# Mixture-of-experts tower: token groups prepared further ahead on four row buffers, and routed sums scattered straight into the output

## The reference

```python
h = h + attention(layernorm(h))          # six layers
x = layernorm(h)
gate_out = x @ gate_w                    # [tokens, 8 experts]
top_v, top_i = jax.lax.top_k(gate_out, 2)
w = softmax over the two chosen, 0 elsewhere
out = sum over experts e of swiglu_e(x) * w[..., e]
out = out + swiglu_shared(x)
h = h + out                              # the result, [16, 256, 256] float32
```

## Time and profile before

| | |
|---|---|
| time, median of 3 runs | 1619.01 us (1618.17 to 1622.71) |
| the profiled execution's own time | 1622.01 us |
| its span in the profile | 1620.0 us |
| PE busy in the span | 1302.3 us (80%) |
| DVE, ACT, POOL busy | 1030.0, 829.5, 973.3 us |
| mean granted TensorE clock | 0.906 of full speed |

### The profile page before, as it was taken

One profiled execution on the slowest core, in us unless ns is written; L12 is line 12 of the kernel. 1 busy time (PEld: TensorE's weight loads), 2 busy tenths in 40 slices (PEclk: granted clock), 3 DMA queues, 4 the chain that ended last, 5 costly groups with the idle time before them and its releaser, 6 DMA issues. The chain is left out here.

```text
span 1620.0 us, 37722 instructions
## 1 busy us (share of the span) xinstructions
PE 1302.3 (80%) x11400; PEld 1107.4 (68%) x11401; DVE 1030.0 (64%) x2634; ACT 829.5 (51%) x2251; POOL 973.3 (60%) x967
## 2 busy tenths in 40 slices
PE   3610189999999999999999996376467999999993
PEld 2510168888888888888888885355355888888883
DVE  3245578888888888888888884343334444444441
ACT  2232168778778777777777774233421223222230
POOL 0047689889889889988988872233443233333332
PEclk8655599999999999999999997778778999999997
DMA  9988323252252242234223243232434244444454
GB/s 328 398 303 284 93 60 65 65 126 63 63 126 62 65 123 68 65 90 101 65 65 91 65 75 56 56 76 66 97 95 137 48 66 66 65 59 59 65 66 123
DMA packets 357115, 166.54 MB, mean 103 GB/s; under 512 B 282241, under 2 KB 340609, under 8 KB 356993
## 3 DMA queue, kind: packets, MB, share of 16 engines
q1 hardware_dynamic: 322210, 124.02, 30.7%
q0 software_dynamic: 20064, 27.14, 9.6%
q10 hardware_dynamic: 14784, 14.68, 2.6%
HBM read 50.27 MB, written 48.66 MB: 61 GB/s over the span
## 5 line engine op out<-in xcount | busy, mean ns | idle before, releaser
L704 PE MATMUL bank<-hT,Wc 128*128 128x256 f16 x2304 | 284.6, 274 | 111.4 <-DMA hT<-hhl 107.0
L704 PEld LDWEIGHTS bank<-hT,Wc 128*128 128x128 f16 x2304 | 226.2, 98 | 139.1 <-issue 112.1
L667 POOL DMA_INDIRECT acc_rows<-h0b,payin x78 | 121.3, 1556 | 239.8 <-DVE h0b L1352 227.9
L799 PE MATMUL bank<-xTg,W12h 128*128 128x256 f16 x1248 | 187.3, 273 | 0.0
L1293 DVE SCALAR_TENSOR_TENSOR gT<-bank,silu 128x512 f32<-128x512 f32 x110 | 76.0, 691 | 170.7 <-ACT silu L1020 170.6
L586 POOL TENSOR_TENSOR h0b<-h0b,rows 128x512 f32<-128x512 f32 x96 | 121.9, 1270 | 94.0 <-issue 47.3
L1020 ACT ACTIVATE silu<-bank 128x512 f32<-128x512 f32 x110 | 65.5, 595 | 217.1 <-PE bank L799 204.5
L704 PE MATMUL bank<-Wc,MT 128*128 128x256 f16 x1152 | 144.0, 276 | 7.8 <-DVE MT L1159 7.8
L704 PE MATMUL bank<-khl,eqT 128*128 128x256 f16 x1152 | 143.9, 275 | 6.3 <-DMA eqT<-EQhl 0.6
L815 PE MATMUL bank<-W3h,gThl 128*128 (+1 forms) x880 | 129.6, 279 | 23.8 <-DVE gThl L1299 18.6
L704 PE MATMUL bank<-Wc,hT 128*128 128x256 f16 x1152 | 142.6, 274 | 0.0
(11 more groups left out here) (153 smaller groups left out, 2913.5 us busy)
## 6 DMA issues: line engine op xcount, KB each, us to landing
VW<-in_L_tok_W SPq DMA_DIRECT2D x28, 512.0 KB, 6.4
FST<-in_L_ffn_ew SPq DMA_DIRECT2D x24, 512.0 KB
emb_rows<-h0b ACTq DMA_DIRECT2D x14, 512.0 KB, 8.7
emb_rows<-VR ACTq DMA_DIRECT2D x14, 512.0 KB, 9.8
Wc<-Wn SPq DMA_DIRECT2D x48, 128.0 KB, 2.2
Wst<-in_L_attn_w_qkv SPq DMA_DIRECT2D x6, 768.0 KB, 4.9
h_rows<-X SPq DMA_DIRECT2D x4, 1024.0 KB, 4.5
X<-h_rows POOLq DMA_DIRECT2D x8, 512.0 KB, 6.1
```

Of the source, the lines that this page charges most:

```text
L667: pool.indirect_dma_start(out=acc_rows, out_offset=bass.IndirectOffsetOnAxis(ap=got(j % PAYS, w, 0, i32), axis=0), in_=yout[j % 2][:, w, : ...
L704: last = mm(to, lhs(a, k, o), moving, start=(i == 0 and k == 0), stop=(i == 2 and k == 1))
L799: last = mm(to, cols((W12h, W12l)[a], e, k, w * HID + (2 * half + c) * P, P), moving, start=(n_ == 0), stop=(n_ == 5))
```

## The change

- There are four row buffers (`ROWS = 4`) beside three for transposes.
- `stats_of` 0 to 5 move behind DVE's share of items 90 to 95, `stats_of(6)` and `(7)` into group 0 of the shared stage. `high` 0, 1 and 2 move behind ACT's share of items 92, 93 and 94 (before: 0 and 1 behind 93 and 95), and `high(g + 3)` stands where `high(g + 2)` stood, but between the two halves of item 2g.
- POOL issues `add_h0` 0 to 4 at once where it issued 0 and 1, and does the rest of the preparation earlier too.
- `gates_of(g + 2)` closes PE's turn of group g.
- The routed sums go by indirect accumulating DMAs with a bounds check straight to the output (`out_rows`), into which `start_out` (formerly `start_acc`) writes the shared result. `acc_rows`, its padding write and the four copies are gone.

```diff
-        xrow, xT = [None] * RING, [None] * RING
+        xrow, xT = [None] * ROWS, [None] * RING
+        xrow[3] = sb("xrow3", [P, GT, ROW], f32, ffn)
...
# sync
                 sp.wait_ge(s_fxlo, g + 1)
-                if g == 2:
-                    sp.wait_ge(s_gate, 1)
                 if g >= RING:
                     sp.wait_ge(s_h12, 4 * (g - RING + 1))
...
-            def start_acc(g):
+            def start_out(g):
...
             sp.wait_ge(s_sadd, 32 * PAIRS)
-            flat = out.rearrange("b s d -> (b s) d")
-            for g in range(4):
-                at = slice(g * TOK // 4, (g + 1) * TOK // 4)
-                sp.dma_start(flat[at, :], acc_rows[at, :]).then_inc(s_out, 16)
-            sp.wait_ge(s_out, 64)
...
# gpsimd
-            add_h0(0)
-            add_h0(1)
+            for g in range(5):
+                add_h0(g)
             root(0)
+            root(1)
             low(0)
-            add_h0(2)
-            root(1)
+            root(2)
             low(1)
-            for g in range(NG):
-                if g + 2 < NG:
-                    root(g + 2)
-                    if g + 3 < NG:
-                        add_h0(g + 3)
-                    low(g + 2)
+            add_h0(5)
+            root(3)
+            low(2)
+            root(4)
+            add_h0(6)
+            root(5)
+            add_h0(7)
+            low(3)
+            scatter_x(0)
+            root(6)
+            scatter_x(1)
+            low(4)
+            root(7)
+            for g in range(2, NG):
                 scatter_x(g)
+                if g + 3 < NG:
+                    low(g + 3)
...
                 for w in range(2):
-                    pool.indirect_dma_start(out=acc_rows, out_offset=bass.IndirectOffsetOnAxis(ap=got(j % PAYS, w, 0, i32), axis=0),
-                                            in_=yout[j % 2][:, w, :], in_offset=None, compute_op=ALU.add).then_inc(s_sadd, 16)
+                    pool.indirect_dma_start(out=out_rows, out_offset=bass.IndirectOffsetOnAxis(ap=got(j % PAYS, w, 0, i32), axis=0),
+                                            in_=yout[j % 2][:, w, :], in_offset=None, compute_op=ALU.add,
+                                            bounds_check=TOK - 1, oob_is_err=False).then_inc(s_sadd, 16)
...
# tensor
             gates_of(0)
+            gates_of(1)
             up_shared(0, 0)
             ranks(0)
-            gates_of(1)
             up_shared(0, 1)
             up_shared(1, 0)
-            ranks(1)
             down(0, 0, E)
             up_shared(1, 1)
+            ranks(1)
+            gates_of(2)
             for g in range(1, NG):
-                if g + 1 < NG:
-                    gates_of(g + 1)
                 up_shared(2 * g, 0)
                 down(2 * g - 1, 1, E)
                 up_shared(2 * g, 1)
...
                 up_shared(2 * g + 1, 1)
+                if g + 2 < NG:
+                    gates_of(g + 2)
...
# scalar
-                if g >= RING:
-                    act.wait_ge(s_scat[g % RING], 16 * TOPK * GT * (g // RING))
+                if g >= ROWS:
+                    act.wait_ge(s_scat[g % ROWS], 16 * TOPK * GT * (g // ROWS))
...
-            item_loop(act, one, 2, prepare=True, behind={ITEMS - 3: lambda: high(0), ITEMS - 1: lambda: high(1)})
+            item_loop(act, one, 2, prepare=True, behind={ITEMS - 4: lambda: high(0), ITEMS - 3: lambda: high(1), ITEMS - 2: lambda: high(2)})
...
+            high(3)
             share_exp(0)
...
             for g in range(1, NG):
                 if g + 1 < NG:
                     share_exp(g + 1)
                 gate(2 * g, 0, 0)
+                if g + 3 < NG:
+                    high(g + 3)
                 gate(2 * g, 0, 1)
-                if g + 2 < NG:
-                    high(g + 2)
...
# vector
-            item_loop(dve, one, AHEAD, behind={ITEMS - 4: lambda: stats_of(0), ITEMS - 3: lambda: stats_of(1)})
+            item_loop(dve, one, AHEAD, behind={ITEMS - 6 + g: partial(stats_of, g) for g in range(6)})
             add(ITEMS - 1)
...
+            stats_of(6)
             choose(0)
...
-            stats_of(2)
+            stats_of(7)
...
-                if g + 2 < NG:
-                    stats_of(g + 2)
                 gate(2 * g + 1, 0)
```

More of the change, by code:

```diff
@@ L7 @@
 from contextlib import ExitStack
+from functools import partial
 import numpy as np
@@ L67, in tower @@
     slot_x = nc.dram_tensor("slot_x", (E * CAP + W2, ROW), f32, kind="Internal").ap()
-    acc_rows = nc.dram_tensor("acc_rows", (TOK + W2, D), f32, kind="Internal").ap()
+    out_rows = out.rearrange("b s d -> (b s) d")
     h0_rows = nc.dram_tensor("h0_rows", (TOK, D), f32, kind="Internal").ap()
@@ L156, in tower @@
         Wn = sb("Wn", [P, 2, WL], f16, att)
+        hhl = [sb(f"hhl{i}", [P, 2, TB, D], f16, att) for i in range(2)]
+        rows = sb("rows", [P, 2, 3, D], f32, att)
         Wc = sb("Wc", [P, 2, WL], f16, att)
-        rows = sb("rows", [P, 2, 3, D], f32, att)
         xn = h0b[:, 0, 0:TB, :]
@@ L494, in _ @@
             sp.wait_ge(s_table, 1)
-            sp.wait_ge(s_pad, 16 * (2 + E))
-            for r in range(RING):
-                sp.wait_ge(s_scat[r], 16 * TOPK * GT * len(range(r, NG, RING)))
+            sp.wait_ge(s_pad, 16 * (1 + E))
+            for r in range(ROWS):
+                sp.wait_ge(s_scat[r], 16 * TOPK * GT * (NG // ROWS))
             def load_pair(j):
@@ L615, in add_h0 @@
                 x4 = slice(GT * g, GT * (g + 1))
-                pool.dma_start(X[:, x4, :], h0v[:, x4, :], accum_op=ALU.add).then_inc(s_h0add[g % RING], 16)
+                pool.dma_start(X[:, x4, :], h0v[:, x4, :], accum_op=ALU.add).then_inc(s_h0add[g], 16)
             def root(g):
@@ L953, in high @@
                 if g == 2:
+                    for landing in s_hT:
+                        act.wait_ge(landing, 8 * ITEMS)
+                if g == 3:
                     act.wait_ge(s_gate, 1)
-                if g >= RING:
-                    act.wait_ge(s_scat[g % RING], 16 * TOPK * GT * (g // RING))
-                    act.wait_ge(s_xT[g % RING], 16 * GT * (g // RING))
-                A(xhl(g % RING, 0), h0b[:, g % 2, :, :], ACT.Copy).then_inc(s_fxhi, 1)
+                if g >= ROWS:
+                    act.wait_ge(s_scat[g % ROWS], 16 * TOPK * GT * (g // ROWS))
+                    act.wait_ge(s_xT[(g - ROWS) % RING], 16 * GT * ((g - ROWS) // RING + 1))
+                A(xhl(g % ROWS, 0), h0b[:, g % 2, :, :], ACT.Copy).then_inc(s_fxhi, 1)
             def one(t, p, prep):
@@ L1313, in _ @@
             rank(0)
+            gate(0, 1)
             choose(1)
-            gate(0, 1)
             gate(1, 0)
-            rank(1)
             share(0, 0)
             gate(1, 1)
-            stats_of(2)
+            rank(1)
+            stats_of(7)
             for g in range(1, NG):
```

48 lines of the change are left out of this document (24 added, 24 removed).

## The result

| | kernel before | changed kernel |
|---|---|---|
| median | 1620.25 us (1618.17 to 1622.71, 4 runs) | 1551.72 us (1548.99 to 1553.85, 4 runs) |
| ratio | | 0.9576, 95% interval 0.9554 to 0.9597 |
| profiled execution | 1622.01 us | 1553.85 us |
| span | 1620.0 us | 1552.1 us |

The changed kernel is 68.5 us faster. The forecast was 1524 with a range to 1553: the sign and the forecast mechanism hold, the size was 28 us too large, and most of that lies in one place. In later sets of runs both kernels were faster, the one before 1603.6 and the changed one 1520.3 us, so each experiment is compared with the kernel before that was timed beside it.

What follows compares the result with a forecast made beforehand. The prediction took instruction order in the shared stage, a closed ring of 31.2 us per group with no engine full, as the bound. Terms +14 - 95 + 0 - 14.5 = -95.5 gave a forecast of 1524 us, range 1503 to 1553.

Steps and rivals of the forecast that it cites:

- attention's end: Between items 90 and 91 DVE waits for `add_h0(0)`, then transposes meet adds: +14 us, bounds +8 and +26.
- first gates to last ranks: Shared stage: cutting the ring of statistics, transposes and ranks takes it from 218.8 to 124 us, -95.
- rival 2: Shared stage: scatters, `low`, `high` and transposes form a ring again, turns of some 24 us: 1552 us. Chance 0.12.
- Its sign of being wrong: Shared stage: turns over 20 us, with waits for `xT` or for a scatter; then the time is above 1535.
- the term is -88: Shared stage gain instead of -95 if PE's 7.2 us starvation for no visible reason comes again.
- The turn: Shared stage, middle group: 17.0 us of PE work plus a 1.4 us stall for `gThl`, 18.4 us.
- Groups 0 and 1: Start of the shared stage: group 0 takes 19 us and group 1 takes 21, with DVE still behind.
- rival 1: Attention: the wait at its end is hidden, or adds don't hinder transposes: 1510 us. Chance 0.10.
- The tail: Program's end: SP's copies, 2.8 us, and the 11.7 us wait behind them both go, -14.5.
- Rival 5: Routed stage: bounds-checked additions make POOL the bound. Chance 0.03 for slower, 0.02 for 1575 us.
- The SBUF rival: The same as rival 3: shared stage, `low` and `glow` hinder each other, 1534 us. Chance 0.08.
- rival 3: Shared stage: POOL's `low` and DVE's `glow` collide, four or five turns losing 2.1 us each: 1534 us. Chance 0.08.

Runs made afterwards that it cites:

- second set: All runs after the first four follow-ups; the kernel before timed there took 1603.6 us and the changed kernel 1520.3 us.
- first set: The main result (1620.25 us before, 1551.72 us changed) together with the first four follow-up runs.
- the pauses: Changed kernel with two small waited-for POOL fills behind each of the 64 scatters, spacing them about 2.2 us apart: 1540.11 us, ratio 0.9488.
- the turns without a burst: Changed kernel with the scatters of groups 4 to 7 issued together after group 7's ranks, leaving two turns free of scatters: 1568.64 us, ratio 0.9667.
- The run with later statistics: Changed kernel with DVE's statistics of groups 0 to 4 one item later and group 5's behind the last addition: 1522.24 us, ratio 0.9493.
- the run with short pauses: Changed kernel with one small waited-for POOL fill behind each scatter: 1518.93 us, ratio 0.9481.
- the one with plain copies: Changed kernel with scatters of groups 4 to 7 behind the last group and 24 plain SP copies in place of groups 4 to 6: 1541.23 us, ratio 0.9612.
- the run with all three edits: Changed kernel with one fill per scatter, later statistics of groups 0 to 5, and `choose(0)` ahead of `stats_of(6)`: 1518.51 us, ratio 0.9467.
- the first four experiments: Output change alone on the kernel before, 1609.05 us; on the changed kernel late scatters, 1568.64; bursts of four, 1548.72; two fills per scatter, 1540.11.
- the next four: Changed kernel with one fill per scatter, 1518.93 us; plain copies, 1541.23; later statistics, 1522.24; `choose(0)` ahead of `stats_of(6)`, 1514.60.

## Why the prediction was right in kind and too large

By its steps, in us. The last column is the second set; each set goes against the kernel before of its set. Attention's end is counted from the start of item 89's sum into `X` to that of item 95's (57.8 and 63.7 us in the first set, 56.0 and 65.7 in the second), so the rows leave out what lies ahead of it and add up to the change of the span only within 2 us.

| step | forecast | first set | second set |
|---|---|---|---|
| attention's end | +14 | +5.9 | +9.7 |
| first gates to last ranks | 218.8 to 124 | 218.8 to 158.3 | 209.1 to 126.1 |
| last ranks to first routed matmul | 0 | +1.2 | +0.1 |
| routed stage and tail | -14.5 | -12.6 | -10.2 |

**That the range held is luck.** 1551.7 lies 1.3 us inside the upper bound of 1553, and that bound was set for rival 2, which is not what happened; the prediction's own case, 1508 to 1545, was missed. Its sign of being wrong came in part: turns over 20 us and a time above 1535, but without waits for `xT` or for a scatter.

**What failed: PE starved "for no visible reason", 7.2 us, "if it comes again the term is -88".** The prediction took it for something that came once. In the first set it belongs to a burst of scatters, of which each turn has one. The bound beside the term was too small for it: in place of 7.2 us there are 22.0 us on PE alone, and more behind them, by DVE's late `choose` and at half clock (PE is busy 125.4 us with the matmuls that take 112.6 in the second set). Between the two sets the stage differs by 32.2 us (158.3 against 126.1) in the changed kernel, and by 9.8 in the kernel before. Why more in the changed one, as I read it: before, seven waits for `xT` left PE idle during most of each burst (it is busy 2.4 to 3.4 of some 10 us in each of the first six), so that starvation there had little to cost; the change filled that idle time with matmuls. No experiment tested this. The rest of the sum's gain was there, but this stood in its place. That dense scatters were the cause in the first set is shown by the pauses (22.0 us to none) and by the turns without a burst (18.39 and 16.68). How they hold up the other engines, and what made that set prone to it, is not shown. In the second set the stage gains 83.0 us instead of 95, mostly because the kernel before takes 9.8 less there.

**The turn was right.** 17.0 us of PE's work, and 1.4 for `gThl` behind `choose` and `high`: forecast 18.4, measured 18.40, 18.39, 18.39, with a wait for `gThl` of 1.5; group 5 was 17.0 and is 16.68. Rival 2, the ring of 24 us, is refuted, though the first result's 23.2 in the mean looks just like it: `xT` is never waited for, and POOL waits for ACT and DVE, not they for it. Without the timeline it would have passed for shown.

**Groups 0 and 1.** Forecast 19 and 21, measured 21.3 and 24.2 in the second set. In group 0, PE waits 3.0 for the mask behind `stats_of(6)`; with that moved, group 0 takes 18.6. In group 1 the wait for `gThl` is 4.8 in one piece instead of 1.4, 1.25 of it because the `glow` runs into `low(4)`, and PE's 19.4 us are partly at half clock. These 5.5 us are more than the 3 that the sum had for hand-overs and half clock, which is why 124 became 126.1.

**Attention's end.** The wait of 11.6 us is the one forecast. "It then meets adds 2, 3 and 4" failed: by 4.4 us an add the queues were to be busy until 987.5, but the last add landed at 980.4, so `hT` and `eqT` took 3.6 and 2.8 instead of 9.6 and 8.9. The meeting that the kernel before has went away, which gives back part of the wait. From the sum of item 89 to that of item 95, the nine traces with the changed kernel's order there have 63.5 to 66.1 us, and three of before's 56.0 to 57.8: +7.7 in the mean, about the lower bound of +8. This is the larger part of rival 1, and the gates of group 0 come at 1013.06 in the first set, not at about 1023. The run with later statistics shows that the mechanism itself is real: there the transposes do meet the adds, and take back most of what the shorter wait gives: 63.2 us, where the kernel before has 56.0 to 57.8.

The Trainium skill (DMA: Bandwidth & Descriptors, section Queues, rings and completion order) says that an engine takes turns between its queues packet by packet. The run with later statistics agrees: `hT` and `eqT` landed at 974.6 and 981.6, while the adds' traffic went on until some 983, so they were not held back behind all of them. But taking turns gave them no quick way through: 10.5 and 14.8 us, and the -4 that the prediction drew from that sentence is not seen. Beside it the prediction read that both adds had ended when `hT` landed, which is not so: in the trace of before the second add is issued at 964.4 and lands after 11.2 us, at 975.6, and `hT` at 974.8.

**The tail.** -14.5 was the copies' 2.8 and 11.7. Last scatter's start to the end went from 18.7 to 7.2 us, so 3.0 are left: the end comes 7.2 us after that start, where SP could issue the copies after 3.8. What lies in the 3 us the trace doesn't show. Rival 5 is refuted: 1552 against 1555 ns, and the routed stage keeps its pace.

**The SBUF rival.** In turns of 18.39 us `glow` took 0.85 instead of 0.69 us, once a turn, so it cost 0.16, as in the earlier trace rows, not 2.1. But there it starts only 0.30 us before the `low` ends. Where it starts earlier in the `low`, it ends 0.55 us behind it all the same: 1.94 us in group 1 of the changed kernel, 2.12 and 1.65 in the run with short pauses, 2.45 in the one with plain copies. So the mechanism of rival 3 is real, and its cost is what is left of the `low`. What was wrong in the rival was that the two meet in full in every turn. The Trainium skill (SBUF — State Buffer, section SBUF: two separate sides) says that whichever of the two starts first holds the shared ports for the whole instruction, and these rows, in all of which the `low` starts first, agree. The 3.93 us in the run with all three edits are not explained by it alone, as that `glow` starts 0.74 us ahead of the `low`. In the first set no `glow` of the changed kernel took over 0.85, so this has no part in the 28 us.

## What to carry to other kernels

Filling an engine's idle time also fills the time in which something else was hidden: look at what ran during the waits that a change removes (here eight scatters in each), and ask what it does to an engine at work. A stretch of "issue" idle time beside a dense row of indirect transfers may be a rate and not an accident: give it a rival of its own, multiplied by the number of such rows. Look where two-input instructions of DVE meet a long one of POOL that reads SBUF too, and count what is left of the long one. When a turn comes out at the size of a rival, read one turn instruction by instruction before believing the rival.

The lowest ratio of these has the changed kernel with `choose(0)` ahead of `stats_of(6)`: 0.9451, against 0.9475 for the changed one. The intervals overlap, so that it is faster rests on the 2.5 us of the two traces. Where runs look like the first set, pauses are worth a test: 0.9488 against 0.9576 there, and in the second set one fill costs nothing that is clear of noise (1518.93 against 1520.30 us, and 1519.56 against 1514.60).

## What was unexpected of the hardware

- Eight indirect scatters issued 1.27 us apart held up PE, DVE and ACT at once in the first set, from some 5 to 9 us after the first until 1 to 2 us behind the last; 32 in a row held PE for one piece of 20.7 us. 2.2 us apart they did not.
- This came and went between sets of runs while each set agreed in itself within some 0.5%: the unaltered kernels took 1620 and 1552 us, then 1604 and 1520. The number of the chip doesn't tell the sets apart: on chip 7 the kernel before took 1622.0 us beside the first four experiments and 1602.8 beside the next four, and then 1603.6 and 1605.5 on chips 15 and 0. A ratio of the two kernels thus depends on it (0.9576 and 0.9475, with intervals that don't meet).
- Of five accumulating transfers of 512 KB in a row the first landed 6.5 us and the last 18 us after the first was issued, so 2.9 us apart, where one takes 6.1 from issue to landing.
- A `glow` (DVE, both inputs in SBUF) that starts while POOL's `low` runs ends 0.55 us behind it, in each of the traces: it takes 0.85 to 2.45 us instead of 0.69.
- The accumulating scatter costs the same with and without a bounds check (1552 and 1555 ns).
